# Full attention stores its outputs by dimension, and issues each step's value batch as two halves

## What is computed

```python
h = _layernorm(x) * (1 + ca) + sa
q, k, v = ...                      # 16 heads of 16, q and k rotated
scores = einsum('bhqd,bhkd->bhqk', q, k) / sqrt(16)
out = einsum('bhqk,bhkd->bhqd', softmax(scores), v)
x = x + ga * (out @ wo.T)
h = _layernorm(x) * (1 + cb) + sb  # goes to the windowed layers
```

## Time and profile before

| what | us |
| --- | --- |
| median of three runs (lowest, highest) | 4847.93 (4840.43, 4849.11) |
| the profiled execution | 4837.09 |
| its span from the first to the last instruction | 4835.1 |
| around the span | 2.0 |
| full attention (from its first load to its last store), in the span | 256 to 1777 |
| attention_out | 1778 to 1962 |

### The profile page before, as it was taken

The page is one execution under the profiler, slowest core; times in us unless marked ns, Lnnn a source line. Parts: engine busy times, 40 slices in busy tenths (PEclk is TensorE's granted clock), DMA queues, the critical chain, the costliest instruction groups (busy, mean ns, idle before and its releaser), DMA issues. The chain is left out here.

```text
span 4835.1 us, 94881 instructions
## 1 busy us (share of the span) xinstructions
PE 4276.8 (88%) x27610; PEld 2744.2 (57%) x27610; DVE 3590.9 (74%) x7998; ACT 2801.1 (58%) x6209; POOL 1616.5 (33%) x2408
## 2 busy tenths in 40 slices
PE   5869999999999976599999997999799999988998
PEld 2423333333333334477777775888577777766787
DVE  6579888888888949688888784454688888875554
ACT  2438777777777850366666663333566666653333
POOL 2300000000000004455555553433455555545545
PEclk8969999999999998799999997999999999998999
DMA  6933323233233317200000002111100000012221
GB/s 204 367 54 61 60 42 60 46 57 54 48 61 50 52 63 243 72 25 26 24 24 26 24 23 63 44 54 35 49 24 25 25 24 25 25 30 85 68 65 51
DMA packets 368130, 297.05 MB, mean 61 GB/s; under 512 B 65820, under 2 KB 324888, under 8 KB 367648
## 3 DMA queue, kind: packets, MB, share of 16 engines
q1 hardware_dynamic: 367648, 291.11, 24.5%
HBM read 178.74 MB, written 111.21 MB: 60 GB/s over the span
## 5 line engine op out<-in xcount | busy, mean ns | idle before, releaser
L889 ACT ACTIVATE fa_P<-fa_pS 128x512 f32<-128x512 f32 x2048 | 1112.0, 595 | 385.7 <-PE fa_pS L815 337.6
L916 DVE TENSOR_REDUCE fa_mx<-fa_pR 128x2 f32<-128x1024 f32 x1024 | 1205.4, 1221 | 151.3 <-PE fa_pR L796 139.5
L1518 POOL TENSOR_TENSOR wa_pn<-wa_pr,wa_ri 128x512 f32<-128x512 f32 x512 | 700.7, 1369 | 614.0 <-DVE wa_ri L1574 600.4
L815 PE MATMUL fa_pS<-fa_Q,fa_K 50*128 50x512 f32 x2048 | 520.2, 504 | 108.0 <-ACT fa_P L889 77.8
L1454 ACT ACTIVATE wa_pr<-wa_sm,wa_mn 128x256 f32<-128x256 f32 x1024 | 510.4, 501 | 177.5 <-DVE wa_mn L1566 177.5
L1140 POOL TENSOR_TENSOR ao_xn<-ao_xn,ao_mod 128x1024 f32<-128x1024 f32 x16 | 37.6, 2348 | 1663.5 <-DVE ao_xn L1105 1663.5
L830 PE MATMUL fa_pO<-fa_P,fa_V 128*32 128x512 f32 x4096 | 560.1, 620 | 0.2 <-ACT fa_P L889 0.2
L815 PEld LDWEIGHTS fa_pS<-fa_Q,fa_K 50*128 50x128 f32 x2048 | 194.6, 187 | 602.9 <-ACT fa_P L889 543.4
L796 PE MATMUL fa_pR<-fa_K,fa_Q 48*128 48x512 f32 x2048 | 406.8, 451 | 60.6 <-DMA fa_K<-parts_d 38.5
L1306 PE MATMUL wa_pQK<-wa_wqkv,wa_xT 128*128 128x512 f32 x1536 | 419.7, 409 | 5.8 <-DVE wa_qa L1611 5.8
L2012 ACT ACTIVATE ff_gl<-ff_pG,ff_b 128x512 f32<-128x512 f32 x192 | 132.6, 691 | 475.2 <-PE ff_pG L1953 475.2
(11 more groups left out here) (186 smaller groups left out, 7191.8 us busy)
## 6 DMA issues: line engine op xcount, KB each, us to landing
parts_d<-pj_parts SPq DMA_DIRECT2D x64, 512.0 KB, 5.4
fa_Q<-parts_d SPq DMA_DIRECT2D x192, 128.0 KB, 4.5
fa_K<-parts_d SPq DMA_DIRECT2D x192, 128.0 KB, 6.9
v_d<-pj_v SPq DMA_DIRECT2D x16, 1024.0 KB, 8.4
fa_V<-v_d SPq DMA_DIRECT2D x32, 512.0 KB, 8.8
pj_x<-in_L_attn_x SPq DMA_DIRECT2D x16, 512.0 KB, 7.6
fa_Q<-fa_nrow SPq DMA_DIRECT2D x512, 2.0 KB
att_d<-fa_att SPq DMA_DIRECT2D x64, 128.0 KB, 2.0
```

The source lines that it names most:

```text
L815: nc.tensor.matmul(pS[:, (s * exped.per + u + e) % T, :], Ks[at:at + SROWS + 2, s, a, kb * P:(kb + 1) * P], Qs[at:at + SROWS + 2, s, a, ha ...
L889: nc.scalar.activation(Pr[:, k % 2, h, :], pS[:, (s * exped.per + u) % T, :], ACT.Exp).then_inc(exped.sem, 1)
L916: nc.vector.tensor_reduce(mx[:, q // QB, :, a, q % QB, kh], row_slot(), AX.X, ALU.max).then_inc(row_free, 1)
L1518: nc.gpsimd.tensor_tensor(pn[:, hp % 2], pr[:, hp % 2], inv, ALU.mult).then_inc(s["weighted"].sem, 1)
```

## The change

- Output path. `sums` results are stored by dimension as they leave ACT: 16 partitions of each head to `num_d`, and the four rows of softmax sums to `den_d`, five DMAs for a half instead of one. No transposes of the sums on PE and no `divide` on DVE. Once both halves of a group have landed, SP loads its sums as 128x32, DVE inverts them (`invert`), and SP stores them to `inv_d`.
- SP's order in a group n becomes `load(n+2)`, `store(n-1, 1)`, a wait for both stores of n-1 to have landed, `max_rows(n, 1)`, `load_sums(n-1)`, `store_inverse(n-1)`, `store(n, 0)`, `max_rows(n+1, 0)`.
- DVE runs `invert(n-1)` in its own order behind the row maxima of step 6.
- Maxima. They keep their sign, POOL splits them into two parts, one transpose turns both parts into a buffer of `pS` (steps 2 and 10 instead of 0 and 8), and ACT copies them out (`max_out`) as one more tile in its order.
- PE's order. A step is scores (a=0), a row tile, the values of step k-1 for queries 0 to 255 of the half, scores (a=1), a row tile, the values for queries 256 to 511.
- At the start the first loads wait for their own memset instead of all three, and the first maxima are turned after all 32 row tiles of group 0 instead of after 16.
- `attention_out` has no transposes on PE and no copy on ACT: POOL multiplies the loaded 128x1024 numerators with the inverse sums, which are loaded broadcast over the dimensions (0.5 MB more for a chunk), and in every second chunk `wo` with the gate (128x512). DVE's gate multiplication is gone, and the sum of x and the product is one DVE operation out of PSUM, which has two buffers.

```diff
+PV_PARTS = 2
...
+    TURN_LATE, TURN_EARLY = 2, KB + 2
+    SLOTS = STEPS * GH + 2
...
+                return n * SLOTS + local(n, TURN_LATE, GH)
+            return 0 if is_first(n) else (n - 1) * SLOTS + local(n - 1, TURN_EARLY, GH)
...
-                        sp.wait_ge(scored.sem, scored.upto(n - NB))
+                        sp.wait_ge(scored, tile(n - NB, STEPS - 1, GH))
...
-                    sp.wait_ge(row_free, max_use(n, half) + 1)
+                    sp.wait_ge(exped, turn_tile(n, half) + 1)
...
-                    sp.wait_ge(row_free, sums_use(n, half) + 1)
...
-                    dst = att_d[bass.ds(b, 1), half * HALF:(half + 1) * HALF, bass.ds(g * (GH * HD), GH * HD)]
-                    sp.dma_start(dst.rearrange("b (k p) c -> p (b k) c", p=P),
-                                 att[:, half]).then_inc(stored[half].sem, 16)
...
+                    sp.wait_ge(o_out.sem, o_out.upto(n, half + 1))
+                    for h in range(GH):
+                        dst = rows_[:, h * HD:(h + 1) * HD].rearrange("g c b t -> (g c) (b t)")
+                        sp.dma_start(dst, OT[h * 32:h * 32 + HD, half, :]).then_inc(stored[half].sem, 16)
+                    dst = den_d[bass.ds(b, 1), bass.ds(g * GH, GH), cols]
+                    sp.dma_start(dst.rearrange("b h t -> (b h) t"),
+                                 OT[HD:P:32, half, :]).then_inc(stored[half].sem, 16)
...
+                def sums_stored(n):
+                    for half in range(2):
+                        sp.wait_ge(stored[half].sem, stored[half].upto(n))
+
+                def load_sums(n):
+                    sp.dma_start(den[:], sums_of(den_d, n)).then_inc(den_in.sem, 16)
+
+                def store_inverse(n):
+                    dst = sums_of(inv_d, n)
+                    sp.wait_ge(inverted.sem, inverted.upto(n))
+                    sp.dma_start(dst, inv[:]).then_inc(inv_out.sem, 16)
...
+                for n in range(2):
+                    sp.wait_ge(ones, n + 1)
+                    load(n, n)
                 sp.wait_ge(ones, NB)
-                load(0, 0)
-                load(1, 1)
                 max_rows(0, 0, 0)
 
                 def body(n, s):
-                    max_rows(n, s, 1)
                     if not (isinstance(n, int) and n + 2 >= GROUPS):
                         load(n + 2, (s + 2) % NB)
                     if not is_first(n):
                         store(n - 1, 1)
+                        sums_stored(n - 1)
+                    max_rows(n, s, 1)
+                    if not is_first(n):
+                        load_sums(n - 1)
+                        store_inverse(n - 1)
+                    store(n, 0)
                     if not is_last(n):
                         max_rows(n + 1, (s + 1) % NB, 0)
-                    store(n, 0)
...
-                    sp.wait_ge(stored[half].sem, stored[half].upto(GROUPS - 1))
+                sums_stored(GROUPS - 1)
+                load_sums(GROUPS - 1)
+                store_inverse(GROUPS - 1)
+                sp.wait_ge(inv_out.sem, inv_out.upto(GROUPS - 1))
...
                 def turn_max(n, half):
-                    pe.wait_ge(neg.sem, neg.upto(n, half + 1))
-                    slot = row_slot()
-                    nc.tensor.transpose(slot[0:MCOLS, 0, 0:P], nm[:, half, :], ident[:]).then_inc(row_full, 1)
+                    pe.wait_ge(top_steps.sem, top_steps.upto(n, 3 * half + 3))
+                    if not (is_first(n) and half == 0):
+                        pe.wait_ge(exped, turn_tile(n, half) - T + 1)
+                    nc.tensor.transpose(pS[0:2 * MCOLS, turn_slot(n, half), 0:P],
+                                        tops[:, half].rearrange("p x c -> p (x c)").bitcast(F32),
+                                        ident[:]).then_inc(scored, 1)
...
-                        pe.wait_ge(exped.sem, n * exped.per + u - 1)
+                    if not (is_first(n) and k == 0 and a == 0):
+                        pe.wait_ge(exped, tile(n, k, 2 * a + 1) - T + 1)
...
+                def sums(n, s, k, part):
+
+                    kb, at = k % KB, part * (HALF // PV_PARTS)
+                    if part == 0:
+                        pe.wait_ge(exped, tile(n, k, GH - 1) + 1)
+                        if k == 0:
+                            pe.wait_ge(v_in.sems[s], v_in.upto(n))
+                            if not is_first(n):
+                                pe.wait_ge(o_out.sem, o_out.upto(n - 1))
+                        if k == KB:
+                            pe.wait_ge(o_out.sem, o_out.upto(n, 1))
+                    cols = slice(at, at + HALF // PV_PARTS)
                     for h in range(GH):
-                        last = nc.tensor.matmul(pO[h * 32:(h + 1) * 32, :], V[:, s, kb, h, :], Pr[:, k % 2, h, :],
-                                                start=(kb == 0), stop=(kb == KB - 1))
-                    last.then_inc(summed.sem, 1)
...
+                        last = nc.tensor.matmul(pO[h * 32:(h + 1) * 32, cols], V[:, s, kb, h, :], Pr[:, k % 2, h, cols],
+                                                start=(kb == 0 and part == 0),
+                                                stop=(kb == KB - 1 and part == PV_PARTS - 1))
+                    if part == PV_PARTS - 1:
+                        last.then_inc(summed.sem, 1)
...
+                for j in range(ROWS):
                     row_scores(0, 0, j)
                 turn_max(0, 0)
-                for j in range(ROWS // 2, ROWS):
-                    row_scores(0, 0, j)
...
                     for k in range(STEPS):
-                        scores(n, s, k, 0)
-                        if not is_last(n):
-                            row_scores(n + 1, (s + 1) % NB, 2 * k)
-                            row_scores(n + 1, (s + 1) % NB, 2 * k + 1)
-                        scores(n, s, k, 1)
+                        before = None
                         if k > 0:
-                            sums(n, s, k - 1)
+                            before = (n, s, k - 1)
                         elif not is_first(n):
-                            sums(n - 1, (s - 1) % NB, STEPS - 1)
-                        if k == 0:
+                            before = (n - 1, (s - 1) % NB, STEPS - 1)
+                        for a in range(PAIRS):
+                            scores(n, s, k, a)
+                            if not is_last(n):
+                                if PV_PARTS == 2:
+                                    row_scores(n + 1, (s + 1) % NB, 2 * k + a)
+                                elif a == 0:
+                                    row_scores(n + 1, (s + 1) % NB, 2 * k)
+                                    row_scores(n + 1, (s + 1) % NB, 2 * k + 1)
+                            if before is not None and (PV_PARTS == 2 or a == 1):
+                                sums(*before, a % PV_PARTS)
+                        if k == TURN_LATE:
                             turn_max(n, 1)
-                        if k == 2 and not is_first(n):
-                            turn_sums(n - 1, 1)
-                        if k == KB and not is_last(n):
+                        if k == TURN_EARLY and not is_last(n):
                             turn_max(n + 1, 0)
-                        if k == KB + 2:
-                            turn_sums(n, 0)
-
...
                     if not is_first(n):
-                        act.wait_ge(row_full, sums_use(n - 1, half) + 1)
+                        act.wait_ge(stored[half].sem, stored[half].upto(n - 1))
                     nc.scalar.copy(OT[:, half, :], pO[:]).then_inc(o_out.sem, 1)
+
+                def max_out(n, s, half):
+                    act.wait_ge(scored, turn_tile(n, half) + 1)
+                    nc.scalar.copy(trow[:, s, half, :], pS[0:2 * MCOLS, turn_slot(n, half), 0:P]).then_inc(exped, 1)
+
+                max_out(0, 0, 0)
 
...
                         if k == 0 and not is_first(n):
                             copy_out(n - 1, 1)
                         if k == KB:
                             copy_out(n, 0)
+                        if k == TURN_LATE:
+                            max_out(n, s, 1)
+                        if k == TURN_EARLY and not is_last(n):
+                            max_out(n + 1, (s + 1) % NB, 0)
...
+                def split(n, half):
+
+                    c = top_steps
+                    pool.wait_ge(c.sem, c.upto(n, 3 * half + 1))
+                    if not is_first(n):
+                        pool.wait_ge(scored, turn_tile(n - 1, half) + 1)
+                    nc.gpsimd.tensor_tensor(tops[:, half, 0, :], top[:, half, :], unit[:],
+                                            ALU.mult).then_inc(c.sem, 1)
+                    pool.wait_ge(c.sem, c.upto(n, 3 * half + 2))
+                    nc.gpsimd.tensor_tensor(tops[:, half, 1, :], top[:, half, :], tops[:, half, 0, :].bitcast(F32),
+                                            ALU.subtract).then_inc(c.sem, 1)
...
+                def invert(n):
```

(46 more changed lines are left out.)

293 lines of the change are left out of this document (113 added, 180 removed).

## The result

| what | us |
| --- | --- |
| before, median of four runs beside it (lowest, highest) | 4848.5 (4840.4, 4865.0) |
| after, median of four runs (lowest, highest) | 5144.9 (5125.5, 5161.2) |
| after divided by before, 95% interval | 1.0605 (1.0557 to 1.0653) |
| after, the profiled execution and its span | 5125.5, 5123.7 |
| full attention in the span, before and after | 1777 - 303 = 1474, 1983 - 303 = 1680 |

The changed kernel is 6% slower. Full attention (counted from 303 us, just ahead of the first scores of group 0, to its last store) takes 206 us more, `attention_out` 107 more, and the rest some 24 less: 206 + 107 - 24 is the 289 by which the spans differ. What made those 24 was not looked for; from the last addition of `attention_out` to the end the profiles of all these kernels take between 2845 and 2897 us, though nothing in those stages was changed.

The account below looks back on a forecast made before the run. No engine is full; a closed loop of 2.69 us per step binds full attention. Full attention +56, start and end +6, attention_out +5 make +67: 4837.1 to 4904, plus 10.8 for the median: 4915, range 4755 to 4975.

Parts of the forecast that it names:

- The steady step, 2.48: Full attention: with values in halves a step takes 2.48 us (2.36 to 2.68) instead of 2.69, including 0.10 per added switch.
- The third rival: Switch from pair tiles to values costs the full 0.21, step 2.68, split gains nothing: +47, 4895 us; chance 0.13.
- The chain on SP: Full attention: maxima writes, then the sums' load, queue on SP behind the store's landing, making step 8 wait.
- S: The moment in a group n when load(n+2) starts; later events of the SP chain are timed from it.
- The two waits, 1.2 and 2.2: At step 8: scores wait 1.2 us for the maxima's DMAs, then row tile 16 about 2.2 for DVE behind the inverse.
- The first rival: The chain on SP isn't late, so every ordinary group gains 3.3 us: -88, 4760 us; chance 0.20.
- Whether the clock falls behind step 8: Full attention: 3.5 us of waits with 0.34 of work drop the clock in each such group, losing 4.0 us.
- The second rival: The chain is late but the clock holds, since the wait falls in two pieces: -17, 4831 us; chance 0.15.
- How long it stays down, 9.4: Full attention: each fall to 1.2 GHz lasts 9.4 us, the mean of the old kernel's eight, losing 4.0 us.
- The last rival: The clock stays low for over 13.6 us in each such group: above 4955, to 5050 us; chance 0.07.
- Groups behind a turn would be 2.5 us shorter than before: Full attention: the eight groups behind a loop turn have no second wait and take 47.6 us instead of 50.1.
- attention_out, +5 between -20 and +27: DVE loses 19.6 us, POOL gains about 47: -20 if none holds DVE up, +27 if all, middle +5.

Follow-up runs that it names:

- whole_at_turns: Changed kernel with the chain_late and ao_ahead edits, plus values whole in steps 0 to 4 behind a loop turn and in group 0: 4762.2 us, ratio 0.9838.
- chain_late: Changed kernel with SP writing turned maxima before load and stores, sums' load and inverse last, DVE inverting behind step 15's maxima: ratio 1.0079.
- ao_ahead: Changed kernel with POOL multiplying the numerators of chunk n+2, not n+1, ahead of its two operations of chunk n in attention_out: 5039.6 us, ratio 1.0393.
- whole_at_8: Changed kernel with values whole in steps 8 to 12 of every group, and 0 to 4 behind a turn and in group 0: 5054.0 us, ratio 1.0427.

## Why the prediction was right or wrong

Forecast 4915 and slower; measured 5145 and slower, above the range. By the steps of the forecast:

- *The steady step, 2.48*: 2.50 measured. The 0.10 for the added switch, which no row showed apart, held: the values start 0.32 behind the row tile, 0.21 of that streaming. *A group without waits, 41.1*: 41.3 and 41.5 in whole_at_turns. The third rival (0.21 for the switch) is refuted by both. TensorEngine Tiling (Array Packing), section Key Properties, of the Trainium skill says that a change of tiling mode drains TensorE; whatever that drain takes is contained in these 0.11 us, which no row divides between it and the weights.
- *The chain on SP*: the maxima at S + 15.9, measured S + 15.6; their last DMA ahead of the sums' load as said; the row tile of step 8 at S + 25.0, measured S + 23.9. *The two waits, 1.2 and 2.2*: 1.5 and 1.6 on average. Each named row is there. The first rival (chain not late) is refuted by the trace, and chain_late shows what the chain cost with its falls: some 255 us.
- *Whether the clock falls behind step 8*: it does. The second rival (it holds, as the wait is in two pieces) is refuted. The row that it and the forecast leaned on, a gap of 1.8 in feed-forward behind which the clock held, was one side of the picture: of the twelve such gaps of the second feed-forward in the profile before, two do have a fall behind them, and in that of after five of twelve. The lines of PE and of the clock behind one of the five, in after:

```profile
4933.47 1.09 PE L1947 MATMUL ff_pH<-ident,ff_hn 128*128 128x128 f32 x8 [1.85 <-DVE ff_hn L1848]
```
```profile
4934.00:4938.00 4.00, 4.00 (x24) 4.00 (x22) 0.59 (x2) 3.35 (x5) 1.29 (x1) 0.59 0.00 0
```

- *How long it stays down, 9.4*: the step that failed. I took the mean of falls behind which PE worked with whole values, and used it for a kernel whose halves stand between the pairs. It was 27.9. The size of a step at the low clock, 4.3, was right (4.32), so the loss is 676 x (1 - 2.50/4.32) = 285 us in all of full attention, against 88 x (1 - 2.69/4.06) = 30 before: 255 more. By the forecast's own figures it would have been 29 x 4.0 - 8 x 3.2 = 90 more. This one term is 165 us of the 230 by which I missed; `attention_out` is another 102, the rest of full attention -15, and the other stages -24. With the step's gain of -106 and waits of some 65 the stage comes to 214, measured 206. The last rival named this case and put 0.07 on it; its time, up to 5050, was passed too, by what `attention_out` lost.
- *Groups behind a turn would be 2.5 us shorter than before*: wrong for the same reason. The one at 978 us, for instance, is followed by 44 us of low clock.
- *attention_out, +5 between -20 and +27*: it was +107. I had added up what DVE loses and POOL gains, as if the busiest engine set the pace. But the product was queued on POOL behind the operations of the chunk two before, so that each engine waited for the next, and a chunk costs the sum of the chain, 17.6. ao_ahead prices it: 105 us by the medians, 90 between the first and the last chunk of the profiles. The bound of +27 assumed that all of POOL's work holds DVE up; PE's 5 to 6 us and DVE's own normalizing stood in the chain too.
- *The rest*: whole_at_8 takes the long falls out and comes to 5054; less the 105 of attention_out it is some 4949. That is 34 above the forecast, with the larger waits and eight gaps for issue that its order added.

## What to carry to other kernels

A wait is priced together with what PE does after it, and a threshold isn't read from one window of a stage when the same gap comes twelve times in it. Before costing a low clock by the falls of the old kernel, see whether the instructions behind the fall are still in the same order, and, where a reordering raises how often PE changes its tiling, use the new order only where no gap comes just before it. When work moves from one engine to another that is idle half of the time, draw the chain of one iteration over all engines before adding up busy times: the place of an operation in its queue decided 90 to 105 us here, its effect on DVE 16. And a gain measured alone (the split: 44 instead of 107) may be hidden by a side effect that can be repaired at a few places.
